# Routed rounds: the high parts of the hidden tiles all on ScalarE, two behind each pair of gelus, and none on GpSimd

## The reference

```python
cur = x                                   # 1024 tokens x 128, after a layernorm
for r in range(4):                        # R rounds
    logits = cur @ Wg[r] + bg[r]          # 4 experts
    vals, idx = top_k(logits, 2)
    w = softmax(vals)
    cw = sum(one_hot(idx, 4) * w[..., None], axis=1)
    hmid = gelu(einsum('nh,ehf->enf', cur, W1) + b1[:, None, :])   # 128 -> 512, all 4 experts
    y = einsum('enf,efh->enh', hmid, W2) + b2[:, None, :]          # 512 -> 128
    cur = cur + einsum('ne,enh->nh', cw, y)
```

## Time and profile before

| | |
|---|---|
| median of 3 runs | 1149.89 us (1145.36 to 1150.44) |
| profiled execution | 1151.09 us, span 1149.3 us, mean granted TensorE clock 0.928 |
| busy share of the span | PE 88%, DVE 70%, ACT 56%, POOL 34% |
| routed rounds | 111.4 to 301.1 us of the span |
| chain that ended last | PE 65%, DVE 14%, ACT 11% |

### The profile page before, as it was taken

One profiled execution on the slowest core, in us unless ns is written; L12 is line 12 of the kernel. 1 busy time (PEld: TensorE's weight loads), 2 busy tenths in 40 slices (PEclk: granted clock), 3 DMA queues, 4 the chain that ended last, 5 costly groups with the idle time before them and its releaser, 6 DMA issues.

```text
span 1149.3 us, 18013 instructions
## 1 busy us (share of the span) xinstructions
PE 1016.8 (88%) x5910; PEld 723.8 (63%) x5910; DVE 804.1 (70%) x1969; ACT 646.1 (56%) x1606; POOL 387.7 (34%) x610
## 2 busy tenths in 40 slices
PE   5597999999769998778999999996899999999677
PEld 4356887888513336556767777775667666768465
DVE  6775789898677862588787786578565566675563
ACT  3163766766317774476787877874144566665121
POOL 7040222111121110336565756577000344444200
PEclk9687999999859998898999999997799999999789
DMA  5712111111052210300000000305101000000000
GB/s 205 138 43 76 66 46 37 37 62 63 29 170 80 80 40 19 147 1 1 1 1 1 1 1 1 147 1 206 58 1 54 22 1 1 1 2 1 0 1 19
DMA packets 32254, 53.55 MB, mean 47 GB/s; under 512 B 4193, under 2 KB 24449, under 8 KB 31009
## 3 DMA queue, kind: packets, MB, share of 16 engines
q1 hardware_dynamic: 29616, 50.03, 13.2%
q10 hardware_dynamic: 2544, 2.36, 0.6%
HBM read 45.33 MB, written 6.88 MB: 45 GB/s over the span
## 4 chain that ended last, share of the span: by engine, by line
PE 65%; DVE 14%; ACT 11%; issue 5%; DMA 2%; POOL 2%; SPq 1%; DVEq 0%; ACTq 0%; POOLq 0%
PE psum L1352 7%; PE psum L1362 7%; PE psum L1698 7%; ACT region_d L1764 4%; PE psum L2358 3%; PE psum L2411 3%; PE psum L2342 2%; PE psum L368 2%; PE psum L412 2%; ACT region_c L1781 2%; PE psum L2325 2%; PE psum L1735 2%; PE psum L1712 2%; PE psum L2320 2%; PE psum L382 1%
## 5 line engine op out<-in xcount | busy, mean ns | idle before, releaser
L1698 PE MATMUL psum<-gated_parts 128*128 128x512 f32 x768 | 197.4, 409 | 15.2 <-DVE region_d L1868 11.0
L1698 PEld LDWEIGHTS psum<-gated_parts 128*128 128x128 f32 x768 | 140.4, 190 | 67.9 <-DVE region_d L1868 31.0
L1949 POOL TENSOR_TENSOR region_d<-region_d 128x256 f32<-128x256 f32 x126 | 99.5, 790 | 112.0 <-DVE region_d L1868 111.7
L1421 ACT ACTIVATE rounds_work<-psum,region_c 128x512 f32<-128x512 f32 x128 | 84.6, 688 | 27.7 <-PE psum L1352 25.6
L797 DVE TENSOR_REDUCE work<-psum 128x1 f32<-128x512 f32 x128 | 81.8, 686 | 21.8 <-PE psum L368 20.4
L1764 ACT ACTIVATE region_d<-psum,gated_work 128x128 f32<-128x128 f32 x256 | 75.8, 450 | 36.8 <-issue 26.2
L1352 PE MATMUL psum<-parts,split 128*128 128x512 f32 x384 | 95.7, 399 | 0.0
L1362 PE MATMUL psum<-parts,split 128*128 128x512 f32 x384 | 93.3, 392 | 0.0
L1868 DVE SCALAR_TENSOR_TENSOR region_d<-psum,gated_work,region_d 128x128 f32<-128x128 f32 x256 | 71.4, 345 | 29.4 <-ACT region_d L1764 23.3
L1475 DVE TENSOR_TENSOR parts<-rounds_work,parts 128x1024 fp32r<-128x1024 f32 x64 | 76.3, 1220 | 16.9 <-POOL parts L1543 15.9
L1868 DVE SCALAR_TENSOR_TENSOR region_d<-psum,ctx,region_d 128x128 f32<-128x128 f32 x256 | 71.4, 344 | 22.7 <-ACT region_d L1764 20.4
(11 more groups left out here) (425 smaller groups left out, 2130.0 us busy)
## 6 DMA issues: line engine op xcount, KB each, us to landing
rounds_work<-cw_rows SPq DMA_DIRECT2D x32, 256.0 KB, 3.4
region_a<-in_l1v SPq DMA_DIRECT2D x8, 512.0 KB, 4.1
region_b_last<-in_l1o SPq DMA_DIRECT2D x1, 4096.0 KB, 12.5
region_a<-in_l2f SPq DMA_DIRECT2D x1, 4096.0 KB, 12.0
region_b_last<-in_l3f_small SPq DMA_DIRECT2D x1, 4096.0 KB, 19.7
region_a<-in_l3f SPq DMA_DIRECT2D x1, 2080.0 KB, 7.4
region_c<-in_l0f SPq DMA_DIRECT2D x1, 2076.0 KB, 12.4
region_c<-in_l3x SPq DMA_DIRECT2D x1, 2048.0 KB, 7.8
```

The costliest lines, as they stand in the source:

```text
L1421: act.activation(H[g % 2][:, f, :], bank[f], ACT.Gelu_apprx_tanh, bias=W("b1")[:, (g % E) * FT + f:(g % E) * FT + f + 1]).then_inc(h_ready ...
L1698: ins = pe.matmul(bank[2 * (n % 2) + c], src[a][:, t * P:(t + 1) * P], weights[b][:, piece(c)], start=m == 0, stop=m == len(PASSES) - 1)
L1949: pool.tensor_tensor(tile[:, 0:2, :], tile[:, 0:2, :], tile[:, 2:4, :], ALU.add).then_inc(k.pool_chain, 1)
```

## The change

ScalarE makes both casts of an item: after gelus 0 and 1 it casts c = 0, after gelus 2 and 3 it casts c = 1. GpSimd's cast is gone; its four memsets stay, each now waiting only for the second gelu of its item. One semaphore, `rounds_h_high`, replaces the two by which VectorE waited for the high parts.

```diff
-    high_pool = k.count("rounds_h_high", ITEMS)
     k.slots_filled = k.count("packed_fill_done", 4)
     FILL_AT = 8
-    high_act = k.count("rounds_high_act", ITEMS)
+    high = k.count("rounds_h_high", 2 * ITEMS)
...
         def hidden(g):
-            for f in range(FT):
-                n = FT * g + f
-                act.wait_ge(*up_psum.at(n + 1))
+            for c in range(2):
+                for f in range(2 * c, 2 * c + 2):
+                    n = FT * g + f
+                    act.wait_ge(*up_psum.at(n + 1))
+                    if g >= 2:
+                        act.wait_ge(*h_low.at(2 * (g - 2) + c + 1))
+                    act.activation(H[g % 2][:, f, :], bank[f], ACT.Gelu_apprx_tanh,
+                                   bias=W("b1")[:, (g % E) * FT + f:(g % E) * FT + f + 1]).then_inc(h_ready.semaphore, 1)
                 if g >= 2:
-                    act.wait_ge(*h_low.at(2 * (g - 2) + f // 2 + 1))
-                act.activation(H[g % 2][:, f, :], bank[f], ACT.Gelu_apprx_tanh,
-                               bias=W("b1")[:, (g % E) * FT + f:(g % E) * FT + f + 1]).then_inc(h_ready.semaphore, 1)
-            if g >= 2:
-                act.wait_ge(*down_psum.at(g - 1))
-            act.wait_ge(*h_ready.at(FT * (g + 1)))
-            act.activation(two(hidden_part[0][g % 2], 1), two(H[g % 2], 1), ACT.Copy).then_inc(high_act.semaphore, 1)
+                    act.wait_ge(*down_psum.at(g - 1))
+                act.wait_ge(*h_ready.at(FT * g + 2 * c + 2))
+                act.activation(two(hidden_part[0][g % 2], c), two(H[g % 2], c), ACT.Copy).then_inc(high.semaphore, 1)
...
         def split_hidden(g):
             for c in range(2):
-                dve.wait_ge(*(high_pool, high_act)[c].at(g + 1))
+                dve.wait_ge(*high.at(2 * g + c + 1))
...
     def gpsimd(pool):
         k.norm.gpsimd(pool, use)
-        for g in range(ITEMS):
-            if g >= 2:
-                pool.wait_ge(*down_psum.at(g - 1))
-            pool.wait_ge(*h_ready.at(FT * g + 2))
-            pool.tensor_copy(two(hidden_part[0][g % 2], 0), two(H[g % 2], 0)).then_inc(high_pool.semaphore, 1)
-            if FILL_AT <= g < FILL_AT + 4:
-                n = g - FILL_AT
-                pool.memset(k.later_slots[n // 2][:, n % 2 * T:(n % 2 + 1) * T], ONES_16)\
-                    .then_inc(k.slots_filled.semaphore, 1)
+        for n in range(4):
+            pool.wait_ge(*h_ready.at(FT * (FILL_AT + n) + 2))
+            pool.memset(k.later_slots[n // 2][:, n % 2 * T:(n % 2 + 1) * T], ONES_16)\
+                .then_inc(k.slots_filled.semaphore, 1)
```

## The result

The changed kernel takes 1166.19 us in the median (1163.71 to 1166.83, 6 runs) against 1150.16 (1145.36 to 1150.98, 6 runs): a ratio of 1.0151, 95% interval 1.0133 to 1.0168. It is slower by 16 us where 8 were forecast, and the time lies above the range of 1152 to 1164. The profiled execution took 1165.84 us with a span of 1164.0 and a mean clock of 0.921.

A forecast was written before the change was run, and what follows sets the result against it. The prediction took PE as the bound, busy 188.67 of 189.66 us. Waits of 6 x 1.28 = 7.7, plus 1.2 at the start, less 0.9 in turn 2, gave +8.0: 1149.89 + 8.0 = 1157.9 us, range 1152 to 1164.

The forecast's parts named there:

- the chain from tanh to route: In each turn, tanh, gelus, casts, subtraction and combine on ACT and DVE precede PE's route step; period forecast 24.64 us.
- its slack of 0.5 us: Before the change the combine ends at 236.78 and the route step starts at 237.34, leaving about 0.5 us.
- the place of the new wait: PE waits at the route step for the last combine, 1.28 us at route steps 2 to 7, 7.7 us in all.
- old stall: In turn 2 PE already idles 0.89 us behind DVE; the longer chain covers it, a term of -0.9 us.
- slow block: Down product behind a route step at fallen clock, 4.45 to 4.6 us against 3.0; forecast only in a rival, at 5.0.
- The start: Route step 1 waits for the copy of the weights, moved from 119.10 to 120.32: a term of +1.2 us.
- the tail: After route step 7 ACT's extra us eats up the 1.4 us before the low part of c = 1 is needed: 0.
- ScalarE's item: ACT's time for one item with four gelus and two casts, not held by PE: forecast 4.64 us.
- the unseen gaps between gelu and cast: Cast between two gelus of one item, and gelu right behind a cast, not in the trace: 0.09 us taken each way.
- ScalarE's busy time: A sign for the changed kernel's profile: ACT busy some 162 us in the stage.
- Clock falls: Rival, chance 0.08: gaps of 1.3 us each turn drop PE's clock, 6 x 2.3 = 14 us more, about 1172.
- the bounds of the gaps between gelu and cast: 0.03 us ahead of a cast gave +5.7 us; less overlap behind casts, 0.21 more at five places, gave +14.7.

The follow-up runs named there:

- e2_act_at_3_0: The changed kernel, with ScalarE casting c = 0 only in items e = 3 and e = 0 and GpSimd in the others: 1164.7 us, ratio 1.0141.

## Why the prediction was wrong

**What held.** PE as the bound, the chain from tanh to route, its slack of 0.5 us, and the place of the new wait were right: waits at line 1372 for line 1506, five of 1.24 us, forecast 1.28, and one of 0.74 in turn 2, which has its old stall beside it. A turn without a slow block takes 24.67 us, forecast 24.64. The start costs +1.1 (1.2), turn 2 covers its old stall (24.65 against 24.26), and the tail costs nothing (-0.1). That is 1.1 + 6 x 1.3 - 0.8 - 0.1 = 8.0 us, the forecast sum. ScalarE's item of 4.61 us against 4.64 shows that the unseen gaps between gelu and cast were taken rightly from the neighbouring rows. By the figures of the Trainium skill's page "ScalarE: Activation LUTs", section "What ACT_TABLE_LOAD costs", the prediction's estimate was 0.07 to 0.1 more, thus 4.71 at least: the trace decides for the rows. Of the signs that were named, ScalarE's busy time missed, 153.7 us in the stage where some 162 were forecast, without bearing on the chain.

**What failed.** The step was the rival "Clock falls", which I gave 0.08 and kept out of the sum, on the ground that "behind the 0.89 us gap at 181 the clock stayed 1.00". The row is right, but it is of a gap two thirds as long as the ones I forecast, and it stands ahead of the transposes and not ahead of a route step. The runs show in its place, at the route steps: with five gaps of 0.80 us no slow block, with six of 1.14 three, with five of 1.24 three in each of three profiles, with five of 1.6 three. The size was off too, the other way: I took 5.0 us for a slow block and one behind each gap, 14 us; it was 4.45 to 4.6 against 3.0, behind half of the route steps. The term is 3 x 1.6 = **4.8 us**, and cutting the gaps alone (five matmuls in each) gave back 4.7 us in the stage and 6 us of the time. By the Trainium skill, page "TensorE: Matmul & The Clock Gate", section "A second HAM failure mode: psum-queue depth-cycling", small frequent pauses between groups of matmuls make the clock swing: for gaps of 1.14 to 1.6 us at the route steps the trace agrees (down products of 4.3 to 4.6 us), for 0.80 us it doesn't.

**What was missing.** The layers behind the stage had no term at all. They take 847.1 us in the mean of three profiles before and 850.1 of three after, +3.0. With 12.8 in the stage this is 15.8. That it comes so near the 16.0 between the medians is partly luck: the stage starts at 109.6, 106.9 and 109.3 us before and at 107.0, 107.6 and 109.2 after, 0.7 earlier in the mean, and the spans of the three profiles differ by 14.9. A part of the +3.0 comes from where the clock rises: a late rise was seen in two of three profiles of the changed kernel and in none of three of the kernel before, but also in two experiments with the casts of the kernel before. The time and the mean clock of the six timed runs fit it, though only the first of them has a trace: five lie at 1165.84 to 1166.83 us and 0.921 to 0.922, as the two profiles with the late rise do, and one at 1163.71 us and 0.926. Why the changed kernel meets it more often stays open, as does what else moves those layers by 1 to 2 us in either direction. Counting on it from the kernel before was not possible, since its one trace doesn't show that they vary.

**The range.** It came from the bounds of the gaps between gelu and cast, with which an item came out within 0.03 us, and left out the clock. Of the two terms that I had not put in, 4.8 and 3.0, neither alone would have left the range (1157.9 + 4.8 = 1162.7); together they did.

## What to carry to other kernels

An engine with a third of its time free can still be on the chain that ends each turn. Follow that chain instruction by instruction through each engine's order, and look first at which waits stand behind work that they don't need: here the combine behind a subtraction, and swapping two steps took back 14.5 of 16 us. When such a chain makes PE wait, price the wait twice, once for itself and once for the clock behind it, and compare it with gaps in the trace that are at least as long and stand ahead of the same work; a shorter one proves nothing, and a single one little.

## What the hardware showed that was not expected

A gap of 0.80 us on PE ahead of a route step, every 24.7 us, left the clock at 1.00 five times of five. One of 1.24 us brought the twelve matmuls behind the route step from 3.0 to about 4.6 us in three of five, in three executions out of three, and one of 1.6 us did so no more often; one of 1.41 us ahead of the transposes did not. Filling a gap with matmuls made the kernel faster by 6 to 8 us.

A GpSimd cast of 1.04 us made VectorE steps beside it longer: 0.17 to 1.05 us for a tensor_scalar of 128x4, which ended with the cast, and 0.69 to 1.10 for an addition of 128x512, which ended 0.5 us behind it. It did not touch all of them: in `e2_act_at_3_0` a reduction that started at 200.59, inside the cast of 200.54 to 201.58, took its 0.17 us as ever.
